# Graph network on one core: in the convolution pass, the low parts of the sources are issued two batches ahead of the rows, and every fourth batch's are kept from the gate pass

## The reference

```
x = layernorm(x + L0(x))   # mean of the neighbours, then a matmul
x = layernorm(x + L1(x))   # messages with a maximum over the edges
x = layernorm(x + L2(x))   # gated graph convolution (this case)
x = layernorm(x + L3(x))   # attention over the edges
```

```
h = gelu(concat(x[row], x[col]) @ mlp_w1 + mlp_b1);  edge_weight = sigmoid(h @ mlp_w2 + mlp_b2)
deg = segment_sum(edge_weight (and 1 for the loop), col);  dinv = rsqrt(deg)
norm = dinv[row] * edge_weight * dinv[col]
out = segment_sum((x @ conv_w)[row] * norm, col) + conv_b
```

## Time and profile before

| | |
|---|---|
| median of 3 runs | 6658.26 us (6647.23 to 6663.53) |
| the profiled execution | 6670.73 us, span 6669.0 us |
| busy share of the span | PE 53%, DVE 52%, ACT 24%, POOL 59% |
| mean granted TensorE clock | 0.64 |
| moved by DMA | 1015.40 MB, 152 GB/s over the span |
| gate pass, about | 3010 to 4345 us |
| convolution pass | 4347 to 4870 us |

### The profile page before, as it was taken

The page is one execution under the profiler, slowest core; times in us unless marked ns, Lnnn a source line. Parts: engine busy times, 40 slices in busy tenths (PEclk is TensorE's granted clock), DMA queues, the critical chain, the costliest instruction groups (busy, mean ns, idle before and its releaser), DMA issues. The chain is left out here.

```text
span 6669.0 us, 85454 instructions
## 1 busy us (share of the span) xinstructions
PE 3561.5 (53%) x19032; PEld 2752.0 (41%) x19032; DVE 3479.4 (52%) x6921; ACT 1575.8 (24%) x3699; POOL 3955.5 (59%) x4526
## 2 busy tenths in 40 slices
PE   3433332245455555554667676766644676666661
PEld 2222222233333333333555555656633555555451
DVE  4444222225566666653666666778854444444445
ACT  1011000131111111131222222267740111111115
POOL 6666556655565655546666666488865555555552
PEclk6565565567777777775555555588876656666665
DMA  5555445424555555524555555489944555545552
GB/s 172 160 157 153 136 150 154 131 82 145 153 162 154 162 156 155 158 80 123 140 138 142 139 140 138 122 262 290 289 140 140 155 152 150 154 150 152 149 152 54
DMA packets 804105, 1015.40 MB, mean 152 GB/s; under 512 B 230791, under 2 KB 509457, under 8 KB 803988
## 3 DMA queue, kind: packets, MB, share of 16 engines
q1 hardware_dynamic: 454068, 466.36, 23.3%
q0 software_dynamic: 144320, 323.10, 18.7%
q10 hardware_dynamic: 205600, 224.71, 9.7%
HBM read 652.13 MB, written 361.61 MB: 152 GB/s over the span
## 5 line engine op out<-in xcount | busy, mean ns | idle before, releaser
L503 POOL DMA_INDIRECT L_gath<-tab_kv,src x832 | 787.4, 946 | 681.3 <-DVE L_pv L1294 428.1
L503 POOL DMA_INDIRECT L_gath<-tab,src x832 | 807.6, 971 | 572.0 <-DVE L_sent L846 324.7
L503 POOL DMA_INDIRECT L2a_gath<-tab_h,src x832 | 787.7, 947 | 481.0 <-issue 435.7
L503 POOL DMA_INDIRECT L_gath<-in_x,src x832 | 787.5, 947 | 475.4 <-issue 235.6
L638 ACT ACTIVATE L_back<-L_pB 128x512 f32<-128x512 f32 x624 | 365.6, 586 | 1386.7 <-remote 830.4
L621 DVE TENSOR_TENSOR_SCAN L_acc<-L_mask,L_acc,L_pT 128x512 f32<-128x512 bf16 x207 | 264.4, 1277 | 696.9 <-remote 640.0
L609 PE MATMUL L_pB<-ident,L_acc 128*128 128x128 f32 x2496 | 501.8, 338 | 232.0 <-issue 116.9
L609 PEld LDWEIGHTS L_pB<-ident,L_acc 128*128 128x128 f32 x2496 | 390.1, 178 | 412.7 <-issue 407.8
L1216 PE MATMUL L_pR<-L_pv,L_same 128*128 128x132 f32 x1664 | 375.4, 390 | 287.1 <-issue 130.6
L958 PE MATMUL L2a_pZ<-w_M,L2a_hid 64*128 64x1 f32 x1664 | 386.1, 350 | 244.1 <-DVE L2a_z L999 201.9
L958 PEld LDWEIGHTS L2a_pZ<-w_M,L2a_hid 64*128 64x128 f32 x1664 | 370.0, 325 | 344.2 <-issue 278.2
(11 more groups left out here) (286 smaller groups left out, 7599.6 us busy)
## 6 DMA issues: line engine op xcount, KB each, us to landing
run<-L_back ACTq DMA_DIRECT2D x416, 256.0 KB
L_seed<-seed SPq DMA_DIRECT2D x416, 256.0 KB
run<-L_back ACTq DMA_DIRECT2D x208, 264.0 KB
seed<-L_zeros SPq DMA_DIRECT2D x208, 256.0 KB
sent<-L2a_gath ACTq DMA_DIRECT2D x208, 256.0 KB
L_sent<-sent SPq DMA_DIRECT2D x208, 256.0 KB
run<-L_back SPq DMA_DIRECT2D x208, 256.0 KB
L_mask<-same SPq DMA_DIRECT2D x208, 128.0 KB
```

What stands on the lines that cost most here:

```text
L503: gp.indirect_dma_start(out=gath[k][:, t, :], out_offset=None, in_=table, in_offset=bass.IndirectOffsetOnAxis(ap=g["src"][:, tile:tile + 1 ...
```

## The change

In the convolution, SyncE's stages get other lags: the low part is issued at lag 0, the rows at 2, the mask at 3, the store at 10 (before: 0, 0, 1, 8). For every fourth batch (slot 0) no low part is loaded: `hot` reads it from `kept_low`, a tile of 52 x 512 bf16 per partition that SyncE fills during the gate pass, with one 128 KB broadcast in each round of four batches (`keep_low`, lag 2), and a wait for all of them at the pass's end. The tiles `lane`, `row` and `high` are made at the start of the gate pass instead of at the start of the convolution; the gate's row iota serves for both. The five tiles live outside both passes and are freed before the node stage.

```
-        with nc.sbuf_tensor("ew_sb", [P, TILES], F32) as ew:
-            edges_gate(nc, g, ew)
-            edges_conv(nc, g, ew)
-            nodes(nc, g, 2, out)
+        with ExitStack() as both:
+            for name, shape, dtype in (("ew", [P, TILES], F32), ("kept_low", [P, BATCHES // SLOTS, BE], BF16), ("lane", [P, 1], F32),
+                                       ("row", [P, HIGH], BF16), ("high", [P, TILES], F32)):
+                g[name] = both.enter_context(nc.sbuf_tensor("c_" + name, shape, dtype))
+            edges_gate(nc, g, g["ew"])
+            edges_conv(nc, g, g["ew"])
+        nodes(nc, g, 2, out)
...
@@ edges_conv, SyncE
-            pipeline(sp, BATCHES, DEEP, [(0, on_short(mask_load(sp, g["low"], low, s_low, s_hotl))), (0, on_short(load)),
-                                         (1, load_mask), (8, on_short(store_rows(sp, run, back, s_back, s_out)))])
+            load_low = mask_load(sp, g["low"], low, s_low, s_hotl)
+
+            def load_other_low(n, k, r):
+                if k > 0:
+                    load_low(n, k, r)
+            pipeline(sp, BATCHES, DEEP, [(0, on_short(load_other_low)), (2, on_short(load)),
+                                         (3, load_mask), (10, on_short(store_rows(sp, run, back, s_back, s_out)))])
@@ edges_conv, GpSimd
-            gp.iota(lane_i[:, :], [[1, 1]], base=0, channel_multiplier=1).then_inc(s_iota, 1)
-            gp.iota(row_i[:, :], [[1, HIGH]], base=0, channel_multiplier=0).then_inc(s_iota, 1)
-            gp.wait_ge(s_prep, 4)
@@ edges_conv, VectorE
-            v.wait_ge(s_iota, 2)
-            v.tensor_copy(lane[:, :], lane_i[:, :]).then_inc(s_prep, 1)
-            v.tensor_copy(row[:, :], row_i[:, :]).then_inc(s_prep, 1)
-            v.tensor_scalar(work[:, :], g["src"][:, 0:TILES], LO, None, ALU.arith_shift_right).then_inc(s_prep, 1)
-            v.wait_ge(s_prep, 3)
-            v.tensor_copy(high[:, :], work[:, :]).then_inc(s_prep, 1)
-            v.wait_ge(s_prep, 4)
-
             def hot(n, k, r):
-                landed(v, s_low, k, r)
+                if k > 0:
+                    landed(v, s_low, k, r)
                 room(v, s_look, n, SLOTS)
-                v.tensor_scalar(hot_low[k][:, :], low[k][:, :], lane[:, 0:1], None, ALU.is_equal).then_inc(s_hotl, 1)
+                mine = low[k][:, :] if k > 0 else kept_low[:, bass.ds(r, 1), :].rearrange("p a e -> p (a e)")
+                v.tensor_scalar(hot_low[k][:, :], mine, lane[:, 0:1], None, ALU.is_equal).then_inc(s_hotl, 1)
@@ edges_gate, SyncE
-            pipeline(sp, BATCHES, SLOTS, [(0, load_seed), (0, load_same)])
+
+            def keep_low(n, k, r):
+                if k == 0:
+                    sp.dma_start(g["kept_low"][:, bass.ds(r, 1), :], g["low"][bass.ds(n * BE, BE)].unsqueeze(0).unsqueeze(0).to_broadcast([P, 1, BE])).then_inc(s_kept, 16)
+            pipeline(sp, BATCHES, SLOTS, [(0, load_seed), (0, load_same), (2, keep_low)])
+            sp.wait_ge(s_kept, 16 * BATCHES // SLOTS)
@@ edges_gate, GpSimd and VectorE
+            gp.iota(lane_i[:, :], [[1, 1]], base=0, channel_multiplier=1).then_inc(s_iota, 1)
...
-            v.wait_ge(s_iota, 1)
+            v.wait_ge(s_iota, 2)
             v.tensor_copy(row, row_i[:, :]).then_inc(s_row, 1)
+            v.tensor_copy(g["row"][:, :], row_i[:, 0:HIGH])
+            v.tensor_copy(g["lane"][:, :], lane_i[:, :])
+            v.tensor_scalar(work[:, :], g["src"][:, 0:TILES], LO, None, ALU.arith_shift_right).then_inc(s_prep, 1)
+            v.wait_ge(s_prep, 1)
+            v.tensor_copy(g["high"][:, :], work[:, :])
```

More of the change, by code:

```diff
@@ L652, in edges_conv @@
         slot = lambda name, shape, dtype=F32: [ph.sb(f"{name}{k}", shape, dtype) for k in range(SLOTS)]
-        mask, low = [ph.sb(f"mask{k}", [P, SLOTS * BE], U8) for k in range(DEEP // SLOTS)], slot("low", [P, BE], BF16)
+        mask, low = [ph.sb(f"mask{k}", [P, SLOTS * BE], U8) for k in range(DEEP // SLOTS)], [None] + [ph.sb(f"low{k}", [P, BE], BF16) for k in range(1, SLOTS)]
         sent, scaled, back = (slot(n, [P, BT, D]) for n in ("sent", "scaled", "back"))
@@ L657, in edges_conv @@
         part = [ph.sb(f"part{k}", [P, BT, HIGH]) for k in range(2)]
-        high = ph.sb("high", [P, TILES])
-        work = ph.sb("work", [P, TILES], I32)
-        lane_i, lane, row_i, row = ph.sb("lane_i", [P, 1], I32), ph.sb("lane", [P, 1]), ph.sb("row_i", [P, HIGH], I32), ph.sb("row", [P, HIGH], BF16)
+        kept_low, lane, row, high = g["kept_low"], g["lane"], g["row"], g["high"]
         pT = [ph.ps(f"pT{k}") for k in range(2)]
@@ L663, in edges_conv @@
         pL = [ph.ps(f"pL{k}") for k in range(2)]
-        s_iota, s_prep, s_hotl, s_hoth, s_look, s_part, s_scale, s_turn, s_scan, s_ret, s_back, s_sum, s_mgo = (ph.sem(n) for n in
-            ("iota", "prep", "hotl", "hoth", "look", "part", "scale", "turn", "scan", "ret", "back", "sum", "mgo"))
+        s_hotl, s_hoth, s_look, s_part, s_scale, s_turn, s_scan, s_ret, s_back, s_sum, s_mgo = (ph.sem(n) for n in
+            ("hotl", "hoth", "look", "part", "scale", "turn", "scan", "ret", "back", "sum", "mgo"))
         s_low, s_sent, s_out = (ph.slot_sems(n, SLOTS) for n in ("low", "sent", "out"))
@@ L904, in edges_gate @@
         nought = ph.sb("nought", [P, ONE], BF16)
-        row_i = ph.sb("row_i", [P, P], I32)
+        row_i, lane_i, work = ph.sb("row_i", [P, P], I32), ph.sb("lane_i", [P, 1], I32), ph.sb("work", [P, TILES], I32)
         deg, left = ph.sb("deg", [P, NT]), ph.sb("left", [P, HIGH])
@@ L915, in edges_gate @@
         s_same, s_seed = (ph.slot_sems(n, SLOTS) for n in ("same", "seed"))
-        s_aside = ph.slot_sems("aside", DEEP)
+        s_aside, s_kept, s_prep = ph.slot_sems("aside", DEEP), ph.sem("kept"), ph.sem("prep")
         aside = g["sent"].rearrange("(p t) f -> p t f", p=P)
```

## The result

The changed kernel took 6584.24 us (median of 4 runs, 6573.33 to 6596.95) beside 6660.9 us for the kernel before (4 runs): ratio 0.9888 [0.9864, 0.9913], some 75 us less. Faster was the likeliest side in the forecast; the gain forecast was 47 us, and 6584 lies just outside the range's lower end, 6588. It is the time given for rival C: the DMA engines fill up and GpSimd paces.

The account below looks back on a forecast made before the run. The prediction held the convolution bound by a ring ending in the low part's landing, with DMA next. 49.3 + 1.7 - 4 = 47 us off 6670.73 gave 6623.7, as a median 6611 us; range 6588 to 6645.

Parts of the forecast that it names:

- rival C: Convolution: DMA engines fill altogether and GpSimd paces, 75 us less at most, 6583 to about 6588 us; chance 0.12.
- The ring through the low part's landing: Convolution: low-part landing, compare, scaling and SyncE's order take 9.82 us for four batches, 2.455 us each, which is the pace.
- The mask: Convolution: loaded once in four batches ahead of a low part in SyncE's order, so VectorE waits about that often.
- The lead's own wait: SyncE's new order: low part of s needs `hot` of s-4, with rows and a store queued behind; costed at nothing.
- Which floor is next: Convolution: DMA engines become the bound at 2.249 us a batch, above GpSimd's 2.132 and VectorE's 2.065; gain 49.3 us.
- no DMA limit at all: Convolution, upper end of the gain: GpSimd's floor of 2.132 us a batch sets the pace, 73.6 us gained.
- A quarter of the low parts gone: Convolution: four batches move 2688 instead of 2816 KB, lowering the DMA floor from 2.262 to 2.159 us a batch.
- Preparation moved: Convolution's start: first `hoth` starts earlier and first `hot` needs no load; 1.7 us gained, from 0 to 3.8.
- The gate: Gate pass: 52 more loads of 128 KB cost 4 us, from 0 to 26; pace stays 6.12 us, share 0.55.
- The clock: Convolution, sign to look for: TensorE's granted clock over 0.95 of the 2.4 GHz level; wrong if it falls.
- Rival E: Slower: TensorE's clock stays at 0.50, 72 us more, 6730, or gate rounds lengthen by 1.4 us; chance together 0.05.
- Stores keep their order relative to the rows: Convolution, SyncE's queue: only the low part moves; rows, mask and store keep their mutual order, with no cost given.

Follow-up runs that it names:

- the fastest run with all 2816 KB: Kernel before with the new lags alone, GpSimd marking three of four tiles and eight result-row buffers, nothing kept from the gate: 6485.68 us, 0.9852.
- the run in which VectorE was busy all the time: Changed kernel with GpSimd marking three of four tiles and eight instead of four result-row buffers: 6479.94 us, 0.9843 of the kernel before.

## Why the prediction came out as it did

- *The bound.* Right. The ring through the low part's landing held the pass; taking it away took the waits of `hot`, and neither fewer bytes (kept quarter alone, 1.0016) nor less GpSimd work (0.9995) did. The mask was named as why the wait falls once in four batches; it accounts for half of the ring's price, and without it the waits are shorter and not rarer.
- *The lead's own wait*, costed at nothing: 0.3 us in 350. Right.
- *Which floor is next.* This is the step that failed: "The engines don't reach that: the best 10 us that I looked at held 0.96. 2.159 / 0.96 = 2.249 us. This is the highest floor and I take it". The share of 0.96 came from a kernel whose demand had gaps; with the ring gone, the share was 1.00. The trace of the kernel before held the warning. Two of its stretches, in the columns of rows 2:

```profile
4571.53:4572.50 0.97, 0.97 (x8) 0.97 (x6) 0.97 (x2) 0.00 (x0) 0.97 (x3) 0.50 1.02 380
...
4574.45:4575.43 0.98, 0.98 (x11) 0.97 (x11) 0.98 (x4) 0.86 (x4) 0.98 (x3) 0.88 0.53 181
```

A share of 1.02 at 380 GB/s stands 2 us from one of 0.53: a mean over 10 us has the gaps in it. And 2.262 us of full engines a batch was taken as a constant of the bytes. It isn't: share times pace after the change is 0.97 x 2.118 = 2.054 us where 2.159 was reckoned, and GB/s divided by share goes from 290 / 0.91 = 319 before to 335 after, 341 and 351 in the runs above; in rows 7 alone it is 342 / 0.93 = 368 and 195 / 0.76 = 257. In place of 2.249 us by DMA the pass ran at 2.118, which is GpSimd's floor (2.132 in the forecast), level with the stores' ring.
- *The mis-sized term.* "Gain: (2.486 - 2.249) x 208 = 49.3 us" and 1.7 us of start were 51 together; measured 521.8 - 445.3 = 76.5. The end of the bounds that I had written down as "no DMA limit at all", 73.6, plus the start gives 75.3. It had a chance of 0.12, which was too little: both kinds of evidence against it came from the stalled kernel. The range was also drawn across its own rival: it was to take in C, whose time was 6583 to 6588, and ended at 6588.
- *A quarter of the low parts gone*: the term lowered a floor that did not bind. 0.9888 with it and 0.9888 without it, and by itself 4 to 16 us slower than before.
- *Preparation moved.* The first `hoth` starts at 4329.04 as `hot` does at 4329.01, without the cast ahead of it; but the second `hot` waits 3.1 us for the first loaded low part. The steady pace accounts for all of the 76.5 us, so what the start gave is nothing within some 2 us, and 1.7 is neither borne out nor refuted.
- *The gate*, 4 us: between 0 and 16, so the term stands within what the runs can tell. Its pace was 6.15 for the 6.12 forecast, its share 0.55 as said. One ground for it was weak: of GpSimd's 345.9 idle us, 310.5 are put down to "issue", and even gathers that wait for nothing stand 1.25 us apart, which is 735 of the 900 us for 588 of them. The time to catch up in is nearer 165 us.
- *The clock*: 0.98, above the 0.95 named. Rival E did not come: the lower mean went with the stalls (0.86 before, 0.87 and 0.89 in the two runs in which the old ring's pace stayed).
- *What I did not see*: the second ring. "Stores keep their order relative to the rows" is true, and yet with pace at 2.12 the stores' ring (2.10) stands level with GpSimd. It cost the forecast nothing here, since both floors are 2.12; for the next step it would have.

## What to carry to other kernels

A resource's share in a kernel that stalls elsewhere is a floor for what it can give, not a ceiling: to price it as the next bound, try the lower bound where it doesn't limit at all and give that case its due chance. When a stall is a ring (buffers, a landing, the order of one issuing queue), look for the other rings through the same queue before naming what comes next, and count them in us a batch beside the engines' floors. Where two floors are level, lowering one shows nothing, which clears neither; lower each alone, and both together. And run a change's parts one by one: here one line of lags did all of it.

## What the runs showed of the hardware that I had not expected

The 16 DMA engines' busy time for the same mix of transfers is not fixed: the same 2816 KB in four batches went at 319 GB/s per full share in the stalled kernel, at 341 when the pace was 2.12 us, and at 351 (358 / 1.02) when it was 2.01. The share reached 1.00 well before the rate stopped rising, and a share of 1.02 shows that it adds up the packets' times and has no end at 1.00. By the packets in the traces of the same stretches, one of 2 KB took 98 ns on the mean before, 92 in the lead alone and 89 in the fastest run with all 2816 KB: the packets themselves became shorter. Why is not shown. GpSimd's mark hardly changed beside engines that were fuller: 559 ns on the mean before, 561 after, 575 in the run in which VectorE was busy all the time.
